# A graph block with three-part float32 products: node order phase, block, graph in the column tiles, and normalisation moved to ScalarE

## The reference, cut to what matters

```
h   = relu(layernorm(x))                        # per node
a1  = relu(bn1(conv1(h)))                       # 128x128 product per node
c   = bn2(conv2(a1))                            # along the nodes: 17 taps, each a 128x128 matrix, padding 8
x_conv = relu(c + h)
s   = h @ w_se.T + b_se                         # 3 numbers per node
A   = exp(-|s_n - s_m|^2) * adj
x_nmp  = A @ relu(h @ w_msg.T + b_msg)
out = x + GRU([x_conv, x_nmp], h)               # gates from w_ih (256 inputs) and w_hh (128 inputs)
```

## Time and profile before

| | |
|---|---|
| median of 3 runs | 337.67 us (337.13 to 338.13) |
| the profiled execution | 337.86 us, of which the span from first to last instruction is 336.1 |
| PE busy | 304.8 us (91%) |
| DVE busy | 277.2 us (82%) |
| ACT busy | 152.0 us (45%) |
| POOL busy | 29.7 us (9%) |
| matmuls | 2041, of which conv2 984 (three for each of 328 shifts) |
| mean granted clock of TensorE | 0.954 |
| DMA | 14.87 MB, 52144 packets, 34548 of them under 512 bytes |

### The profile page before, as it was taken

The page is one execution under the profiler, slowest core; times in us unless marked ns, Lnnn a source line. Parts: engine busy times, 40 slices in busy tenths (PEclk is TensorE's granted clock), DMA queues, the critical chain, the costliest instruction groups (busy, mean ns, idle before and its releaser), DMA issues.

```text
span 336.1 us, 5716 instructions
## 1 busy us (share of the span) xinstructions
PE 304.8 (91%) x2041; PEld 278.7 (83%) x2041; DVE 277.2 (82%) x654; ACT 152.0 (45%) x250; POOL 29.7 (9%) x35
## 2 busy tenths in 40 slices
PE   5808883989999999999999999999999999999991
PEld 4708773977999899989998899889998999899880
DVE  7999977389898989898989898998989896847345
ACT  1545532446454555285426543554545652730241
POOL 5733100010001000100001000100010000000000
PEclk9865998799999999999999999999999999999995
DMA  7902100070016000700062003400140002002002
GB/s 224 188 4 38 27 2 0 25 164 2 2 29 161 1 2 0 178 12 0 3 126 65 0 3 65 124 0 2 32 96 0 0 3 62 2 1 64 0 0 64
DMA packets 52144, 14.87 MB, mean 44 GB/s; under 512 B 34548, under 2 KB 51972, under 8 KB 51988
## 3 DMA queue, kind: packets, MB, share of 16 engines
q1 hardware_dynamic: 51518, 13.18, 16.9%
q10 hardware_dynamic: 438, 1.25, 1.2%
q0 software_dynamic: 160, 0.07, 0.4%
HBM read 10.30 MB, written 4.19 MB: 43 GB/s over the span
## 4 chain that ended last, share of the span: by engine, by line
PE 77%; DVE 3%; ACT 2%; issue 1%; DVEq 0%; ACTq 0%
PE bank L886 22%; PE bank L887 21%; PE bank L888 21%; PE bank L956 3%; PE bank L983 3%; PE bank L1039 2%; PE bank L931 2%; PE bank L975 1%; PE bank L966 1%; DVE stats L533 0%; DVE place L676 0%; ACT a_hi L371 0%; ACT edge L395 0%; DVE place L687 0%; ACT a_hi L374 0%
## 5 line engine op out<-in xcount | busy, mean ns | idle before, releaser
L886 PE MATMUL bank<-a_hi,w_hi 128*128 128x256 f32 (+1 forms) x328 | 100.3, 306 | 5.7 <-DVE place L676 5.7
L887 PE MATMUL bank<-a_lo,w_hi 128*128 128x256 f32 (+1 forms) x328 | 96.8, 295 | 0.0
L888 PE MATMUL bank<-a_hi,w_lo 128*128 128x256 f32 (+1 forms) x328 | 96.7, 295 | 0.0
L886 PEld LDWEIGHTS bank<-a_hi,w_hi 128*128 128x128 f32 x328 | 64.6, 197 | 6.5 <-issue 5.9
L887 PEld LDWEIGHTS bank<-a_lo,w_hi 128*128 128x128 f32 x328 | 64.5, 197 | 0.6
L888 PEld LDWEIGHTS bank<-a_hi,w_lo 128*128 128x128 f32 x328 | 64.2, 196 | 0.0
L306 POOL TENSOR_TENSOR rstd<-var_eps,halves 128x8 f32<-128x8 f32 (+1 forms) x9 | 13.6, 1511 | 208.2 <-DVE var_eps L550 208.2
L886 PE MATMUL bank<-h_hi,w_hi 128*128 128x512 f32 (+1 forms) x66 | 26.7, 405 | 1.5 <-DVE ms_b L599 1.3
L363 ACT ACTIVATE a_f<-bank,bn_shift,bn_scale 128x512 f32<-128x512 f32 x16 | 12.5, 785 | 30.6 <-PE bank L888 28.2
L887 PE MATMUL bank<-h_lo,w_hi 128*128 128x512 f32 (+1 forms) x66 | 25.5, 386 | 0.0
L888 PE MATMUL bank<-h_hi,w_lo 128*128 128x512 f32 (+1 forms) x66 | 25.4, 385 | 0.0
(11 more groups left out here) (142 smaller groups left out, 646.2 us busy)
## 6 DMA issues: line engine op xcount, KB each, us to landing
adj_in<-in_adj SPq DMA_DIRECT2D x64, 64.0 KB, 2.3
x_slot<-in_x SPq DMA_DIRECT2D x8, 256.0 KB, 4.0
place<-in_x SPq DMA_DIRECT2D x8, 256.0 KB, 3.9
out<-x_slot SPq DMA_DIRECT2D x8, 256.0 KB, 2.6
out<-place SPq DMA_DIRECT2D x7, 256.0 KB, 2.5
place<-in_L_gnn_conv_w ACTq DMA_DIRECT2D x1, 1088.0 KB, 7.1
place<-in_L_gnn_w_ih SPq DMA_DIRECT2D x1, 384.0 KB, 4.4
out<-place SPq DMA_DIRECT2D x2, 128.0 KB, 2.3
```

The source lines that it names most:

```text
L886: pe.matmul(out, w_hi[:, mat, :], hi, start=start, stop=False)
L887: pe.matmul(out, w_hi[:, mat, :], lo, start=False, stop=False)
L888: final = pe.matmul(out, w_lo[:, mat, :], hi, start=False, stop=stop)
```

## The change

1. **Node order.** Every column tile now has the order phase, block, graph: a node n is 4 v + r, and a half's 512 columns are ordered by r, then v, then the 4 graphs (graph innermost). The tiles `a1_*` become `[D, 9, 2, VPAD * GB]` with VOFF = 1 and VPAD = 34, so a shift by one block moves the operand by 4 floats, and the moving operand is 2 runs (one for each half). Rounding to even is gone, so shifts of 1 or -1 run over 31 blocks where the 32nd is padding.
2. **What reads and writes by graph.** The transposes in (L931) and the aggregation (L983) write PSUM with a step of 4 floats, and the message products (L956) and transposes out (L1039) read their stationary operand with a step of 4 floats (`by_graph`).
3. **Row tiles permuted alike.** `load_x` and `store_y` place node 4 v + r in row r * 32 + v; each becomes four DMAs of 32 partitions.
4. **Adjacency.** `load_adj` still has four DMAs for a half, but each loads, for 32 partitions, the whole of the graphs (pieces of 2048 bytes) at an offset of 3 - i floats; the transposes on DVE then read it with a step of 4 floats.
5. **Normalisation on ScalarE.** `x_normed` is an activation with scale `rstd` and bias `norm_bias`; the bias is computed by a second small operation on GpSimd.
6. **Smaller edits.** `conv_out` is two instructions, one for each half, with contiguous output; `residual` reads contiguous runs; `conv_high` of a half waits for its own half. `edge` shares the memory of `x_norm`. Fewer memsets at the start.

The core of the diff:

```diff
-    VOFF = 2
-    VPAD = VN + 4
-    VC = PB * VN
+    VOFF = 1
+    VPAD = VN + 2
+    VW = GB * VN
+    VC = 2 * VW
...
-        adj_in = [sb(f"adj_in{k}", [N, GB, N]) for k in range(2)]
+        adj_in = [sb(f"adj_in{k}", [N, GB, 4 * N + 4]) for k in range(2)]
...
-        a1_hi = sb("a1_hi", [D, 9, PB, VPAD], F32R)
+        a1_hi = sb("a1_hi", [D, 9, 2, VPAD * GB], F32R)
...
+        def blocks(first, last):
+
+            return slice((VOFF + first) * GB, (VOFF + last) * GB)
...
             def load_x(s, k):
-                sp.dma_start(x_slots[s % 4][:, k * GB:(k + 1) * GB, :],
-                             x[s * PB + k * GB:s * PB + (k + 1) * GB].rearrange("b n d -> n b d")
-                             ).then_inc(x_in[s % 4][k], 16)
+                src = x[s * PB + k * GB:s * PB + (k + 1) * GB].rearrange("b (v r) d -> r v b d", r=4)
+                for r in range(4):
+                    sp.dma_start(x_slots[s % 4][r * VN:(r + 1) * VN, k * GB:(k + 1) * GB, :], src[r]
+                                 ).then_inc(x_in[s % 4][k], 16)
...
+                src = adj[s * PB + k * GB:s * PB + (k + 1) * GB].rearrange("b (c r) m -> c b (r m)", r=4)
+                for i in range(4):
+                    sp.dma_start(adj_in[k][i * QUAD:(i + 1) * QUAD, :, 3 - i:3 - i + 4 * N], src
                                  ).then_inc(adj_in_sem[k], 16)
...
                                    ).then_inc(rstd_ready, 1)
+                pool.wait_ge(rstd_ready, i + 1)
+                pool.wait_ge(mean_ready, i + 1)
+                pool.tensor_tensor(norm_bias[:, graphs], neg_mean[:, graphs], rstd[:, graphs], ALU.mult
+                                   ).then_inc(nbias_ready, 1)
...
+            def x_normed(s, k):
+
+                act.wait_ge(nbias_ready, (k if s == 0 else s + 1) + 1)
+                wait(act, hT_done, 2 * (s - 1) + k + 1)
+                wait(act, edgem_ready, 2 * s)
+                for b in range(k * GB, (k + 1) * GB):
+                    act.activation(x_norm[:, b, :], x_slots[s % 4][:, b, :], ACT.Identity, bias=norm_bias[:, b:b + 1],
+                                   scale=rstd[:, b:b + 1]).then_inc(xnorm_ready, 1)
...
             def conv_high(s, k):
-                act.wait_ge(convf_ready, 2 * s + 2)
+                act.wait_ge(convf_ready, 4 * s + 3 + k)
...
                 gate_z(s, 0)
+                if s + 2 < NP:
+                    x_normed(s + 2, 0)
                 gate_n(s, 0)
+                if s + 2 < NP:
+                    x_normed(s + 2, 1)
                 hh_n_half(s, 1)
...
-                dve.scalar_tensor_tensor(by_pair(conv_f)[:, e], both(bank[B_CB][:, :]), bn_scale[:, 1:2],
-                                         both(pre[e]), ALU.mult, ALU.add).then_inc(convf_ready, 1)
+                to = conv_f[:, half(k)].rearrange("p (q e w) -> p e q w", q=2, e=2)[:, e]
+                product, rest = (ap.rearrange("p (q k w) -> p k q w", q=2, k=2)[:, k]
+                                 for ap in (bank[B_CB][:, :], pre[e]))
+                dve.scalar_tensor_tensor(to, product, bn_scale[:, 1:2], rest, ALU.mult, ALU.add
+                                         ).then_inc(convf_ready, 1)
...
                 for shift in order[first:stop]:
-                    lo = max(0, begin - shift) // 2 * 2
-                    hi = min(VN, (VN - shift + 1) // 2 * 2)
-                    cols = slice(lo + shift + VOFF, hi + shift + VOFF)
+                    lo, hi = max(0, begin - shift), min(VN, VN - shift)
+                    cols = blocks(lo + shift, hi + shift)
...
+            def by_graph(ap):
+
+                return ap[:, :].rearrange("p (n b) -> p b n", b=GB)
...
-                    tr = pe.transpose(bank[B_F[k]][:, b * N:(b + 1) * N], x_norm[:, k * GB + b, :], ident[:, :])
+                    tr = pe.transpose(by_graph(bank[B_F[k]])[:, b], x_norm[:, k * GB + b, :], ident[:, :])
```

More of the change, by code:

```diff
@@ L244, in store_y @@
                 to = slice(s * PB + k * GB + graphs.start, s * PB + k * GB + graphs.stop)
-                sp.dma_start(out[to].rearrange("b n d -> n b d"),
-                             x_slots[s % 4][:, k * GB + graphs.start:k * GB + graphs.stop, :]
-                             ).then_inc(out_done[k], 16)
+                dst = out[to].rearrange("b (v r) d -> r v b d", r=4)
+                for r in range(4):
+                    sp.dma_start(dst[r], x_slots[s % 4][r * VN:(r + 1) * VN,
+                                                        k * GB + graphs.start:k * GB + graphs.stop, :]
+                                 ).then_inc(out_done[k], 16)
             load_x(0, 0)
@@ L435, in _ @@
             weights_high(0)
+            x_normed(0, 0)
+            x_normed(0, 1)
             h_copies(0, 0)
@@ L551, in x_moments @@
                                          ALU.add).then_inc(vareps_ready, 1)
-            def x_normed(s, k):
-                i = k if s == 0 else s + 1
-                dve.wait_ge(mean_ready, i + 1)
-                dve.wait_ge(rstd_ready, i + 1)
-                wait(dve, hT_done, 2 * (s - 1) + k + 1)
-                for b in range(k * GB, (k + 1) * GB):
-                    dve.tensor_scalar(x_norm[:, b, :], x_slots[s % 4][:, b, :], mean[:, b:b + 1], rstd[:, b:b + 1],
-                                      ALU.subtract, ALU.mult).then_inc(xnorm_ready, 1)
             def h_low(t, k):
@@ L668, in residual @@
                 dve.wait_ge(t_ready, s + 1)
-                wait(dve, convf_ready, 2 * (s - 1) + e + 1)
-                dve.tensor_tensor(both(pre[e]), both(t_sum), by_pair(h_f[s % 2][:, :])[:, e], ALU.add
-                                  ).then_inc(h_added, 1)
+                wait(dve, convf_ready, 4 * (s - 1) + 2 * (e + 1))
+                hs = h_f[s % 2][:, :].rearrange("p (k q e w) -> p e q k w", k=2, q=2, e=2)[:, e]
+                sums, ts = (ap.rearrange("p (q k w) -> p q k w", q=2, k=2) for ap in (pre[e], t_sum))
+                dve.tensor_tensor(sums, ts, hs, ALU.add).then_inc(h_added, 1)
             def parity_part(s, e):
@@ L834, in iteration @@
                     result(s - 1, 1, OUT_BANKS[1])
-                conv_out(s, 0)
+                conv_out(s, 0, 0)
+                conv_out(s, 0, 1)
                 if s == 0:
@@ L846, in iteration @@
                     x_moments(s + 3, PB * (s + 3), slice(0, PB))
-                conv_out(s, 1)
+                conv_out(s, 1, 0)
+                conv_out(s, 1, 1)
                 if ahead:
@@ L1034, in gru_products, with out_transposes @@
                     gru_part(N_BANKS, IH + 4, *conv, k, False, True, [part], gru_n_done)
-            def out_transposes(s, k, dst, i=0, cols=slice(0, GC)):
-                pe.wait_ge(gru_ready, 2 * s + k + 1 + i)
-                for b in range(cols.start // N, cols.stop // N):
-                    tr = pe.transpose(bank[dst][:, b * N:(b + 1) * N], z_h[k][:, b * N:(b + 1) * N], ident[:, :])
+            def out_transposes(s, k, dst, graphs=range(GB)):
+                pe.wait_ge(gru_ready, 2 * s + k + 1 + (s == NP - 1 and k == 1))
+                for b in graphs:
+                    tr = pe.transpose(bank[dst][:, b * D:(b + 1) * D], by_graph(z_h[k])[:, b], ident[:, :])
                 tr.then_inc(outT_done, 1)
@@ L1190, in _ @@
             pe.wait_ge(tr_ready, 2 * NP)
-            for (i, cols), dst in zip(column_parts(True), END_OUT_BANKS[1:]):
-                out_transposes(NP - 1, 1, dst, i, cols)
+            out_transposes(NP - 1, 1, END_OUT_BANKS[1], range(GB // 2))
+            out_transposes(NP - 1, 1, END_OUT_BANKS[2], range(GB // 2, GB))
 INPUTS = ["x", "adj"] + ["L0_gnn_" + n for n in (
```

107 lines of the change are left out of this document (46 added, 61 removed).

## The result

The changed kernel takes **353.7 us** (median of 4 runs, 352.8 to 357.8) against 337.9 beside it: ratio 1.049, 95% interval 1.040 to 1.058. The forecast was 330.0 us. The profiled execution took 353.0, with a span of 350.6 us.

A forecast was written before the change was run, and what follows sets the result against it. PE was taken to bound the steady iterations, never waiting, with DVE behind. Steady conv2 -9.8, start +2.1, iteration 0 -0.6 and -0.7, end +1.25 sum to -7.75 us: forecast 330.0 us, range 326 to 336.

The forecast's parts named there:

- Conv2: Conv2 matmuls in the steady part: 15.52 to 14.11 us, -1.4 us an iteration, -9.8 us for iterations 1 to 7.
- main assumption: PE matmuls cost about 1.8 ns per piece of 4 floats touched, so run starts matter, not columns alone.
- PSUM writes: Transposes in and aggregation writing PSUM with a step of 4 floats: taken as 0, at worst +120 ns a pass.
- DVE: DVE work per iteration falls from 31.3 to about 28.6 us of 34.2, staying behind PE.
- A: Rival: stepped PSUM writes at L931 and L983 cost 0.12 us on 192 passes, +23 us, 353 us; chance 0.12.
- C: Rival: conv2 run starts don't matter, eight runs or data kind do; about 338.5 us; chance 0.04.
- D: Rival: DVE or start bind; adjacency transposes double, "b0" waits, start 2 to 3 us later; 332 to 336; chance 0.10.
- stationary operands with a step: Message passes and transposes out loading with a step of 4 floats: taken as 0, far bound +120 ns a load.
- Rival B: Stepped stationary loads of messages and transposes out slow 192 passes, same price as stepped PSUM writes, 353 us; chance 0.04.
- The start: Start: +1.0 late x, +0.3 POOL, +0.8 first adjacency transposes, together +2.1 us (0.5 to 4).
- Iteration 0: Iteration 0: -0.6 us from conv2, -0.7 us from the first half of the last conv_out being ready earlier.
- The end: End: conv_lo wait shrinks by 0.65, more output DMA issues cost +1.9, together +1.25 us.

The follow-up runs named there:

- part 3: Kernel before, every run of the conv2 operands moved down to start at a multiple of 4 floats (wrong taps): 332.5 us, ratio 0.983.
- the kernel with the step of 2: Kernel before, messages' stationary operand read with a step of 2 floats (wrong nodes): 339.7 us in a single run.
- part 4: Changed kernel, messages' stationary operand taken as adjacent columns again (wrong nodes): 343.5 us, then 341.5 us, ratio 1.010 both times.

## Why the prediction was wrong

**Right.** *Conv2*: -1.4 us an iteration was forecast. The changed kernel with adjacent messages runs at 34.28, and without the 0.10 of the transposes out that is -1.47; the price per piece of 4 floats, called the main assumption, held at 118 to 121, 114 and 112 to 113 ns, and part 3 shows that starts count. That part was worth 0.73 us an iteration; the rest of the 1.47 comes with the fewer columns and the fewer pieces of the short matmuls. *PSUM writes*: 0 was right. *DVE*: 29.6 us an iteration (148.17 / 5) against 32.1 before, -2.5 where -2.7 was forecast; behind PE, with no wait before "b0". The residual's two instructions take 1.29 instead of 2.13, the adjacency transposes 1.05 each (0.8 to 1.1 foreseen), the halves of conv_out 0.44. *ACT* in the steady part: no cost. Rivals A, C and D's "b0" are out.

**The step that failed: stationary operands with a step, taken at 0.** It costs 1.92 us an iteration in the messages and 0.10 in the transposes out; the messages alone 12.9 us of the kernel (354.4 to 341.5), more than the whole forecast gain. Rival B was right in its mechanism and too high in its count: transposes out pay a tenth, and step 0's messages nothing. That its 353 us is the time measured is luck: the stepped loads make about 13 of the 22 us between forecast and measured span (14.5 + 7.75), and most of the rest is the start and iteration 0. The argument was rows 5: a stepped load among the weight transposes that showed nothing. Three things were wrong with them as a price.
- They were *transposes*. At full clock the adjacent loads last 141 ns for a transpose and 190 for a message matmul, two lines that stood in the trace before; the stepped ones 210 and 328. What costs nothing for the shorter load says nothing of the longer.
- They stood at the *lower clock*, where such a step shows nothing at all. I noted the clock, and wrote that a load above 107 ns would have shown. The kernel before has four weight transposes that all read with a step of 17 floats (10.27 us). Their groups by line: in the kernel before, where the granted clock is 0.50, the four stepped ones, then four adjacent ones (28.0 us); last the same four stepped ones in the kernel with the step of 2, where the clock is 1.00.

```profile
L1075 PEld LDWEIGHTS bank<-ident,place 128*128 128x128 f32 x4 | 0.9, 230 | 0.0
L1075 PEld LDWEIGHTS bank<-ident,place 128*128 128x128 f32 x4 | 0.8, 228 | 0.0
L1075 PEld LDWEIGHTS bank<-ident,place 128*128 128x128 f32 x4 | 0.6, 214 | 0.1
```

  So 230 against 228 ns at the lower clock, but 214 against 141 at the higher. Adjacent message loads at clock 0.50 take as long as stepped ones at 1.00, and longer (the kernel of part 4 with adjacent columns, 16.9 to 18.5 us, with the window's clock):

```profile
L971 PEld LDWEIGHTS bank<-w_ms,h_f 128*128 128x128 f32 x8 | 1.9, 337 | 0.0
16.80:18.60 1.80, 1.80 (x10) 1.80 (x10) 1.47 (x2) 0.72 (x2) 1.80 (x2) 0.50 1.12 204
```

- The bound, 233 ns a pass, was what came. I held the bound and the Trainium skill's rule against one far row and gave the rival 0.04. With an operand that had no near row, and a price (13 us and more) above the forecast gain, the chance should have been nearer to a half.

**The start: mis-sized.** Forecast +2.1 (0.5 to 4), measured +7.5. The late x, put at 1.0, is 4.3: issues cost 0.53 us each, the upper end I had named, and the second half waits for all eight, which I left out, counting only the first half's. The normalisation on ScalarE was costed at nothing at the start too, although there its cover (gate operations) doesn't exist: 1.65 us a half in the chain from x to PE. The adjacency, +0.8, is 2.2 (variation 1.2). This is the start of rival D (first transposes of step 1 later than 41.5 us), with twice the price that D was given.

**Iteration 0**: forecast -0.6 and -0.7, measured +3.0, of which 1.3 lie above the longest of the runs like the kernel before. Messages undone gave 1.0 and the normalisation 1.8, against a variation of 1.7, and the granted clock in it is 0.89 against 0.92; how the 3.0 divide stays open. The conv_out halves gave nothing there: the 0.9 us wait for conv_lo of the earlier trace rows lies in iteration 0 and not at the end, as I had it, and is 1.2 us after.

**The end**: forecast +1.25. The eight last issues take 3.6 us (row below), and the span ends 4.9 us after the last result instead of 3.4: +1.5, near the +1.9. What I missed is a wait in the diff itself: with the nodes of all graphs mixed, the last transposes need both parts of the gates.

```profile
PE bank L1054 <- DVE place L742: 4.7, 1, 4.7
```

```profile
345.33 3.60 SPq L252 DMA_DIRECT2D out<-place  x8
```

Before, PE waited 3.7 us there and went on with the first two graphs. That is another 1.0; iteration 7's conv2 gave its 1.4 back. With the 0.55 of iteration 6 that makes 1.6, measured 1.4. The 0.65 that I took off at the end for conv_lo had no wait to come from.

## What to carry to other kernels

Before a layout is changed for the moving operand, list every instruction that uses the same tile as its stationary operand, and read its load's duration against its pass: a float32 message load of 190 ns with passes 112 ns apart had no room, and the step that leaves one float in 16 bytes made them 328 and 233. Read such a row at the clock at which the kernel will run: at half the clock the same kind of step showed nothing. When a permutation must be paid somewhere, pay it on the engine with a gap, at a place in its row where it waits (0 us there, 0.8 us an iteration a few instructions earlier). And cost the start by its own chain: a DMA split in four is four issues in a row for all that is queued behind.

## What the runs showed of the hardware

- Stationary float32 load, 128 columns, granted clock 1.00: 190 ns adjacent, 196 with a step of 8 bytes, 328 with 16, in the message matmuls; 141 adjacent, 210 with 16 and 214 with 68 in transposes. Passes 112, 118, 233; 109 and 120 (adjacent and 16).
- The same at granted clock 0.50: transposes 228 adjacent, 230 with a step of 68 bytes; messages 337 adjacent.
- Moving operand: 8 runs of 32 floats cost 130 ns when they start off a multiple of 16 bytes and 119 when on it.
- Writes to PSUM with a step of 16 bytes: no change (8 passes in 1.03 us). ScalarE reads PSUM in permuted order for nothing (0.610 us against 0.613), but SBUF for twice the time (1.196 against 0.624 for conv_hi, adjacent in SBUF); VectorE pays for strided SBUF reads as well (1.09 against 0.68).
- A small VectorE copy (128x3) or normalisation beside a GpSimd row of 1.5 us lasted until that row's end: 1.37 to 2.68 us instead of about 0.2 and 0.34.
- A DMA issue of 32 partitions costs SP about as much as one of 128: 0.53 against 0.49 us.
